# A loop body of six passes instead of one, with each engine's order of three interleaved chains laid out anew

## The reference, cut to what matters

```python
x = patch_embed(images)                       # 197 tokens of 128 features an image
for l in range(2):                            # "front": attention and feed-forward
    h = rmsnorm(x, ln1); q, k, v = h @ wqkv.T
    x = x + softmax(q @ k.T * scale) @ v @ wo.T       # 8 heads of 16
    h2 = rmsnorm(x, ln2); x = x + (silu(h2 @ wg.T) * (h2 @ wu.T)) @ wd.T
x = rmsnorm(x, ln_f)
for d in ("f", "b"):                          # "back": two directions of a scan
    xs = silu(conv4(x @ W_in)); dt = softplus(...); dA = exp(dt * A)   # 128 x 16 states a token
    h[t] = dA[t] * h[t-1] + dt * B[t] * xs;   y = (h * C).sum(states) + D * xs
    out += (y * silu(z)) @ W_out
# layer norm; top-8 routing with room for 256 tokens an expert; the experts; sum
```

## Time and profile before

| | |
|---|---|
| median of 3 runs | 8180.4 us (8171.39 to 8187.01) |
| the profiled execution, its own time | 8183.0 us |
| its span on the core | 8181.2 us |
| busy share of the span | PE 82%, DVE 82%, ACT 76%, PEld 46%, POOL 10% |
| granted clock of TensorE, mean | 0.944 |

### The profile page before, as it was taken

The page is one execution under the profiler, slowest core; times in us unless marked ns, Lnnn a source line. Parts: engine busy times, 40 slices in busy tenths (PEclk is TensorE's granted clock), DMA queues, the critical chain, the costliest instruction groups (busy, mean ns, idle before and its releaser), DMA issues. The chain is left out here.

```text
span 8181.2 us, 116060 instructions
## 1 busy us (share of the span) xinstructions
PE 6725.6 (82%) x33290; PEld 3782.0 (46%) x33290; DVE 6709.8 (82%) x8110; ACT 6220.4 (76%) x13680; POOL 829.6 (10%) x555
## 2 busy tenths in 40 slices
PE   7887877788888888888888888888888888888570
PEld 3444444444444544454444445444444444444240
DVE  2788888888888888888888888888888888888833
ACT  4877767688878887888788878888788878887434
POOL 0144342500000000000000000000000000000075
PEclk8998999999999999999999999999999999999775
DMA  2343333233333333333333333333333333333366
GB/s 98 113 143 122 136 112 116 101 124 136 119 133 124 131 126 133 126 126 131 127 126 124 130 125 126 124 132 123 126 124 136 119 133 126 127 128 123 133 122 203
DMA packets 282797, 1040.75 MB, mean 127 GB/s; under 512 B 37570, under 2 KB 129526, under 8 KB 273824
## 3 DMA queue, kind: packets, MB, share of 16 engines
q1 hardware_dynamic: 248352, 1014.00, 34.6%
q0 software_dynamic: 33792, 21.18, 1.6%
HBM read 955.77 MB, written 90.98 MB: 128 GB/s over the span
## 5 line engine op out<-in xcount | busy, mean ns | idle before, releaser
L880 DVE TENSOR_TENSOR_SCAN hs<-dA,hs 128x1584 f32<-128x1584 f32 x512 | 1766.7, 3450 | 161.7 <-issue 152.8
L1080 PE MATMUL psS<-KM,Q 128*99 128x394 f32 x4096 | 1737.8, 528 | 71.2 <-ACT PTs L622 56.3
L616 ACT ACTIVATE P<-psS,least_s 99x197 f32<-99x197 f32 x4096 | 1469.6, 452 | 146.7 <-DVE least_s L819 138.2
L691 ACT ACTIVATE dA<-dt_,aneg 128x394 f32<-128x394 f32 x2048 | 1207.2, 631 | 164.4 <-DVE hs L880 153.7
L1087 PEld LDWEIGHTS psS<-cst,P 99*99 99x99 f32 x8192 | 945.3, 172 | 822.7 <-ACT P L616 601.7
L1087 PE MATMUL psS<-cst,P 99*99 99x99 f32 x8192 | 1053.7, 262 | 242.2 <-ACT P L616 239.0
L819 DVE TENSOR_REDUCE least_s<-psS 99x2 f32<-99x394 f32 x2048 | 1080.7, 559 | 181.3 <-PE psS L1080 163.6
L622 ACT ACTIVATE PTs<-psS 99x396 f32<-99x396 f32 x2048 | 1012.1, 525 | 276.3 <-PE psS L1087 251.0
L871 DVE TENSOR_TENSOR hs<-hs,u 128x1584 f32<-128x1584 f32 x512 | 921.1, 1799 | 69.2 <-DMA hs<-bc_scratch 69.2
L885 DVE TENSOR_TENSOR hs<-hs,cr 128x1584 f32<-128x1584 f32 x512 | 920.7, 1798 | 0.0
L1172 PE MATMUL psY<-hs,cst 128*128 128x396 f32 x2048 | 779.3, 509 | 123.2 <-DVE hs L889 123.2
(11 more groups left out here) (215 smaller groups left out, 9252.6 us busy)
## 6 DMA issues: line engine op xcount, KB each, us to landing
hs<-bc_scratch SPq DMA_DIRECT2D x512, 792.0 KB, 4.1
cr<-bc_scratch SPq DMA_DIRECT2D x512, 792.0 KB, 5.7
pat<-patches SPq DMA_DIRECT2D x64, 1176.0 KB, 6.9
more_scratch<-zeros SPq DMA_DIRECT2D x64, 197.0 KB, 5.2
rows_scratch<-hs SPq DMA_DIRECT2D x1, 12352.0 KB, 43.0
PTs<-more_scratch SPq DMA_DIRECT2D x24, 512.0 KB, 6.1
sum_scratch<-HW SPq DMA_DIRECT2D x64, 148.5 KB
hs<-rows_scratch SPq DMA_DIRECT2D x24, 386.0 KB, 3.4
```

The lines of the kernel that those rows point to most:

```text
L616: last = nc.scalar.activation(P[:, r, b, m, 0:T], psS[0:CT, 2 * r + b, m * T:(m + 1) * T], ACT.Exp, bias=least_s[:, r, b, m:m + 1], scale= ...
L691: last = nc.scalar.activation(shifted(dA[:, g % 2, k, :]), images(dt_[:, d, :]), ACT.Exp, scale=aneg[:, d, n:n + 1])
L880: nc.vector.tensor_tensor_scan(h, a, h, 0.0, ALU.mult, ALU.add).then_inc(scan_ready, 1)
L1080: mm(psS[0:CT, 2 * r + b, 0:2 * T].rearrange("p (e t) -> p e t", e=2), Q[:, r, b, q * CT:(q + 1) * CT], KM[:, r, h % 2 * 2:h % 2 * 2 + 2, ...
```

## The change

Three edits.

1. The hardware loop's body holds `PASSES = 6` passes. Ten turns of it make the same 60 passes; for SP (`peel=1`) nine turns make 54 and the other nine passes are written out straight. Each of the six passes stands in a loop of its own that runs once (`Fori(0, 1)`), so each ends in a compare-and-branch that is not taken.
2. All lists are rotated, that is, they are cut at another place. ACT's begins with `(2, 'f', 'norm', 1, 1)` now, DVE's with `(1, 'f', 'norm', 0, 1)`, PE's with `(1, 'f', 'down', 0)`. An entry that went from the end of a list to its head has a lag that is one larger, so it is still done for the same step at nearly the same place in the endless sequence.
3. Within the lists entries change places. The set of entries is the same. The larger moves: on DVE `scan 4` stands before the last norm (`norm 1 2`, which writes `H`) and `down 0`; `scan 5` and `half 4` stand before `norm 1 0`; `output 5` goes ahead of the first scores. On PE `sum 4` goes ahead of `norm 0 0`, `sum 5` some eight entries ahead. On ACT `norm 1 0` goes between the two `project` parts. SP's list keeps the order of its transfers (only `conv`, which issues nothing in the loop, moves).

```diff
 HALF = QUARTERS // 2
+PASSES = 6
...
     "dve": [
-        (3, 'b', 'scan', 4), (3, 'b', 'input', 5), (3, 'b', 'output', 4), (1, 'f', 'norm', 1, 0), (0, 'f', 'conv', 0), (3, 'b', 'scan', 5),
-        (3, 'b', 'half', 4), (2, 'b', 'gate', 0), (3, 'b', 'input', 6), (1, 'f', 'score', 1, 0, 0), (0, 'f', 'norm', 0, 0), (1, 'f', 'score', 1, 0, 1),
-        (3, 'b', 'output', 5), (3, 'b', 'scan', 6), (1, 'f', 'score', 1, 1, 0), (1, 'f', 'score', 1, 1, 1), (3, 'b', 'half', 5), (0, 'f', 'score', 0, 0, 0),
...
-        (1, 'f', 'sig', 1), (2, 'b', 'half', 3), (1, 'f', 'up', 1), (0, 'f', 'sig', 0), (1, 'f', 'down', 1), (2, 'b', 'ys', 0), (0, 'f', 'up', 0),
-        (2, 'b', 'input', 4), (1, 'f', 'norm', 1, 2), (0, 'f', 'down', 0),
+        (1, 'f', 'norm', 0, 1), (3, 'b', 'output', 3), (2, 'f', 'sig', 1), (3, 'b', 'half', 3), (2, 'f', 'up', 1), (1, 'f', 'sig', 0), (3, 'b', 'ys', 0),
+        (3, 'b', 'input', 4), (2, 'f', 'down', 1), (1, 'f', 'up', 0), (3, 'b', 'scan', 4), (2, 'f', 'norm', 1, 2), (1, 'f', 'down', 0), (3, 'b', 'input', 5),
+        (3, 'b', 'output', 4), (3, 'b', 'scan', 5), (3, 'b', 'half', 4), (1, 'f', 'norm', 1, 0), (0, 'f', 'conv', 0), (2, 'b', 'gate', 0), (3, 'b', 'input', 6),
+        (3, 'b', 'output', 5), (1, 'f', 'score', 1, 0, 0), (0, 'f', 'norm', 0, 0), (1, 'f', 'score', 1, 0, 1), (3, 'b', 'scan', 6), (3, 'b', 'half', 5),
...
     "act": [
-        (1, 'f', 'norm', 0, 1), (2, 'f', 'sig', 1), (3, 'b', 'decay', 4, 0), (1, 'f', 'gate', 0), (3, 'b', 'decay', 4, 1), (1, 'f', 'sig', 0), (3, 'b', 'decay', 4, 2),
...
-        (0, 'f', 'den', 0), (1, 'f', 'norm', 1, 1), (2, 'b', 'dt', 1), (0, 'f', 'square', 0, 1), (1, 'f', 'gate', 1),
+        (2, 'f', 'norm', 1, 1), (3, 'b', 'dt', 1), (1, 'f', 'square', 0, 1), (2, 'f', 'gate', 1), (1, 'f', 'norm', 0, 1), (2, 'f', 'sig', 1), (3, 'b', 'decay', 4, 0),
...
+        (2, 'b', 'project', 0, 0), (1, 'f', 'norm', 1, 0), (2, 'b', 'project', 0, 1), (3, 'b', 'decay', 6, 0), (2, 'b', 'sigmoid', 0), (3, 'b', 'decay', 6, 1),
...
     "pe": [
-        (2, 'b', 'project', 0, 0), (1, 'f', 'norm', 1, 0), (2, 'b', 'project', 0, 1), (0, 'f', 'conv', 0), (1, 'f', 'qkv', 1), (0, 'f', 'norm', 0, 0),
...
-        (1, 'f', 'up', 1), (2, 'b', 'sum', 3), (1, 'f', 'down', 1), (0, 'f', 'up', 0), (1, 'f', 'norm', 1, 2), (0, 'f', 'down', 0),
+        (1, 'f', 'down', 0), (2, 'b', 'project', 0, 0), (1, 'f', 'norm', 1, 0), (2, 'b', 'project', 0, 1), (0, 'f', 'conv', 0), (1, 'f', 'qkv', 1), (3, 'b', 'sum', 4),
...
@@ -367,9 +367,12 @@
             for p in range(LAGS + 1):
                 run(lambda lag: p - lag, p)
-            with eng.Fori(0, STEPS - peel - LAGS - 1) as n:
-                run(lambda lag: n + (LAGS + 1 - lag), None)
-            for p in range(STEPS - peel, STEPS + LAGS):
+            turns = (STEPS - peel - LAGS - 1) // PASSES
+            with eng.Fori(0, turns * PASSES, PASSES) as n:
+                for k in range(PASSES):
+                    with eng.Fori(0, 1):
+                        run(lambda lag: n + (LAGS + 1 + k - lag), None)
+            for p in range(LAGS + 1 + turns * PASSES, STEPS + LAGS):
                 run(lambda lag: p - lag, p)
```

More of the change, by code:

```diff
@@ L58 @@
 HALF = QUARTERS // 2
+PASSES = 6
 ORDER = {
     "dve": [
[15 rows of a table removed]
[14 rows of a table added]
     ],
     "act": [
[24 rows of a table removed]
[24 rows of a table added]
     ],
     "pe": [
[18 rows of a table removed]
[18 rows of a table added]
     ],
     "sp": [
-        (3, 'b', 'load', 3), (3, 'b', 'share', 1), (3, 'b', 'load', 4), (3, 'b', 'load', 5), (3, 'b', 'load', 6), (2, 'b', 'patch'), (3, 'b', 'load', 7),
-        (0, 'f', 'conv', 0), (2, 'b', 'share', 0), (2, 'b', 'load', 0), (2, 'b', 'load', 1), (2, 'b', 'load', 2), (3, 'b', 'store'),
+        (3, 'b', 'load', 3), (3, 'b', 'share', 1), (3, 'b', 'load', 4), (3, 'b', 'load', 5), (0, 'f', 'conv', 0), (3, 'b', 'load', 6), (2, 'b', 'patch'),
+        (3, 'b', 'load', 7), (2, 'b', 'share', 0), (2, 'b', 'load', 0), (2, 'b', 'load', 1), (2, 'b', 'load', 2), (3, 'b', 'store'),
     ],
```

## The result

| | before | after |
|---|---|---|
| median of 4 runs | 8178.4 us (8171.39 to 8187.01) | 7776.3 us (7771.52 to 7786.64) |
| profiled execution, its own time | 8183.0 us | 7771.5 us |
| ratio, 95% interval | | 0.951 (0.9493 to 0.9526) |

The change takes 402 us off.

A forecast was written before the change was run, and what follows sets the result against it. No engine alone was the bound; branch-back pauses stopped DVE twice a pass, about 5.1 us. 8183 − 253 + 22 + 25 + 6 + 18 = 8001, less 2.6 for the median, 26 more granted: 7975 us, range 7880 to 8115.

The forecast's parts named there:

- The order: Rearranged lists: a new wait where the front chain lags DVE, 0.3 us a pass, +18 us, bounds −60 to +60.
- Fifty fewer edges: Loop's branches back, nine instead of 59: ACT saves 125 us and DVE 128, together 253 us.
- half the gain goes into a new wait: Rival: DVE leaves its pauses sooner but waits for PE's scores and norms; about 8105 us, chance 0.14.
- Each pause is seen in full: First passes' intervals, 126.8, 129.6, 132.5 to 133.1 us with none, one, two edges; 26 us more gain granted.
- The nine edges left: PE's branch back over a body six times as long costs 9 × 2.5 = 22 us, bounds 0 and 23.
- The branch over `route`: Branch skipping `route`, now at six places: PE stops one time in three, 25 us, bounds 0 and 124.
- the inner loops: Register move, addition and untaken branch per engine and pass: 0.1 us each, 6 us, bounds 0 and 18.
- The loads: SP's transfers: same issue order, two buffers freed sooner; zero, bounds −60 and 0.
- No effect: Rival: the inner loops' branches cost as much as the old ones; 8180 us, chance 0.03.
- misses everywhere: Rival: straight code misses at the branch over `route` on every engine, 128 us; about 8100 us, chance 0.10.
- PE starves: Rival: PE, reading 6000 instructions a turn, stops for code within each pass; slower, 8293 us, chance 0.06.
- More gain: Rival: all 305 us from the edges and an order better by 1 us a pass; 7871 us, chance 0.07.

The follow-up runs named there:

- e2: The kernel after with the loop of before (one pass a turn) and the new lists; 7878.5 us, 0.9641 of before.
- e1: The kernel after with the lists of before, keeping the new loop of six passes a turn; 8026.6 us, 0.9813 of before.
- e9: The kernel before with the target of the branch back announced at the head of each turn; 7966.8 us, 0.9745 of before.
- e13: The loop of before (one pass a turn) with the new lists, against e2 with the branch target announced; 7723.4 us, 0.9448 of before.
- e3: Six passes a turn, entries in the sequence of before, lists only cut at the new places; 8019.4 us, 0.9806 of before.
- e8: e3 with only DVE's first 13 entries in the new order, ACT's and PE's lists old; 8084.6 us, 0.9892 of before.
- e12: The kernel after with PE alone on one pass a turn, the other engines on six; 7738.3 us, 0.9458 of before.
- e10: The kernel after with the target of its outer loop's branch back announced; 7731.2 us, 0.9452 of before.
- e15: e3 with scan 1 and half 0 moved ahead of scores on DVE alone; 8041.2 us, 0.9834 of before.

## Why the prediction was wrong, step by step

**The step that failed is "The order"**: "+18 us, bounds −60 to +60". Measured, the new lists are worth −300 with 59 pauses (before to e2), −250 with nine (e1 to after) and −243 with none (e9 to e13). I had seen the waits for a matmul in the earlier trace rows and said that no edit names them. But the edits put `ys`, `input` and `output` exactly ahead of the entries that wait, and the waits of 1.7 us (X) and 1.6 us (scores) a pass are gone (e3 and after). I followed one chain of the new lists, `H` to `qkv`, and not the entries that carried the largest waits. The bound was wrong too: "−1 us a pass, from the size of these waits" is less than any one of the four waits (1.2 to 1.8). Their sum is 6.3 us a pass, 378 us. From before to e2 these four gave 39.5 us in twelve passes, 3.3 of the 5.1 us a pass; the rest came mostly from the waits for ACT's `rs` (37.4 to 24.2) and before `O` (8.2 to 1.9), and from DVE's busy time, which fell from 1200.5 to 1190.6 us; no run tells why.

The part of that step that I did work out held in place and not in size: with all lists moved, PE waits 17.1 us for `H` in twelve passes and no more than 1.7 at once, where I had put 3.4 idle and covered. Without ACT's and PE's moves the early scan costs 65 us (e8), and not by that wait but by DVE's for `rs`.

**"Fifty fewer edges", 253 us**: the loop alone gave 152 (e1). Two causes, both measured. The two pauses of an edge are worth 3.5 us and not 5.1 (e9), 176 us for fifty, and PE's new stops give back 38 (e12, measured with the new lists): 138, and 14 us are not accounted for. The rest of the pauses was hidden: with the pauses gone ACT's `rs` waits for its mean (24.1 us in twelve passes where it was 18.2), and DVE waits before `wo`'s and `conv`'s X, as the rival "half the gain goes into a new wait" had it, but for a third of the 5.1 us and at other entries. With the new lists an edge is worth less again: e2 to e13 is 155 us over 59, 2.6 us each. That explains most of why the halves (152 and 300) come to 50 us more than the whole: 50 × (3.5 − 2.6) = 45.

The two misses pull opposite ways, which is luck: the order gave 268 us more than its +18, and the loop, with all its terms, 74 less than the 226 put down for it (253 and 26, less 22, 25 and 6).

**"Each pause is seen in full", +26 us granted**: wrong for the sixty passes. In the first ones it is nearly so, 4.7 of 5.1 us (e9). But `route` is executed there, and further on, where it is skipped, an edge is worth 3.4. The rest of the 6 us is no edge: e9's second interval is 1 us longer than its first without a pause, and e1's 3 us. The reservation that I wrote down, fuller buffers at pass 3, was not the case: e3's first two intervals are 126.75 and 126.69 us.

**"The nine edges left", 22 us**: right in kind, too small. PE is idle at all nine edges, 2.9 to 3.3 us (27.8 in all, where I had 22), behind a branch of 3.4 to 3.8 us on its sequencer; what e12's expectation says of seven edges is a misreading. The stops are worth 34 to 38 us. The Trainium skill (Runtime: NRT & Kernel Launch, "Instruction fetch mechanics") holds that a taken branch to code outside the loaded window has to fetch it, and that PE's window is the larger one. By that rule PE's edge is free before and paid after, and so the runs show it: the branch takes 0.2 us before and 3.5 after (medians).

**"The branch over `route`", 25 us, and "the inner loops", 6 us**: nearly nothing. Both stand in e10 and not in e13, with 8 us between the two kernels, less than the intervals can tell apart; an inner branch that falls through takes 0.03 to 0.08 us. The stop of the earlier trace rows did not come back: PE's longest wait before a score in the twelve passes is 0.3 us, and its only "issue" idles there are the two edges.

**"The loads", zero**: the wait is 15.3 us in twelve passes, 1.3 us a pass against 1.0. No wait went; it grew a little, by 16 us in sixty passes, where zero was the upper bound.

**The rivals.** "No effect" and "misses everywhere" are excluded by the rows above. "PE starves" too: in the whole run PE's "issue" idles are the nine edges. The Trainium skill (Runtime: NRT & Kernel Launch, "Instruction fetch mechanics") holds that straight fetching hides behind the pace of issue, and these rows agree. "More gain" (7871) had the right sign and its order term of −60 was a quarter of the true one.

The sum with the measured terms: 8178 − 176 (fifty edges) + 38 (PE's stops) − 250 (order with nine edges) = 7790, against 7776. That only closes the account; it uses the same runs.

**What stays open.** Which entries of the tail do it: only e15 was tried, and it did not gain. Why e1's first passes have the longer PE times and the lower granted clock. The granted clock in the twelve passes is 0.98 before and after, 0.97 in e1 and 0.99 in e2, so it is no large part of the difference; PE's busy time there falls from 1213.9 us (e1) to 1195.1, and whether 1% of clock is cause or result was not tried.

## What to carry to other kernels

When lists of several in-order engines change places, go through the waits of the old profile from the largest down and look up for each what the new list puts ahead of the waiting entry; the sum of these waits gives the size that the gain can have (378 us against 300 here, part of which came from other waits), and no single engine's list shows it. A pause behind a branch back is worth what is left on the path when it goes, 3.5 of 5.1 us here, and an interval from a stretch with other work in it (`route` here) is no measure of it. Before unrolling a loop to have fewer edges, try to announce the branch's target: here it removed the pauses that six passes only made rarer, and in e10 all of PE's new stops but one of 1.2 us.

## What was not expected of the hardware

- Announcing the target of the branch back cut the idle behind it on DVE from 2.5 us to 0.1 in the one-pass loop, and ACT's and DVE's pauses vanish from the waits (e9: 208 us for 59 edges).
- PE's branch over a body of six passes takes 3.4 to 3.8 us on its sequencer at all nine edges, and PE's idle is a little shorter (2.9 to 3.3 us). DVE's branch takes 0.06 us, and its idle of 2.9 us stands behind the branch.
